# Sparse attention stage: one-hot places made between maxima and quotients, and scores multiplied ahead of the context products of two sequences back

## The reference, cut to what matters

```python
m = scores_sample.max(axis=-1) - scores_sample.mean(axis=-1)      # from 35 sampled keys
_, top_idx = jax.lax.top_k(m, TOP_U)                              # 35 queries of each head
context = broadcast(v.mean(axis=-2))                              # for every query
scores_top = einsum('bhud,bhkd->bhuk', q_top, k) * scale
attn = softmax(scores_top)
out_top = einsum('bhuk,bhkd->bhud', attn, v)
context = context.at[bi, hi, top_idx].set(out_top)
x = x + context.reshape(b, l, d) @ Wo.T + bo
```

## Time and profile before

| | us |
|---|---|
| median of 3 runs | 2660.38 (2650.34 to 2662.59) |
| the profiled execution | 2671.16, its span 2669.4 |
| PE, DVE, ACT, POOL busy in the span | 2088.6, 1658.7, 1593.7, 726.9 |
| the loop of the sparse attention, first gather to last `add` of the loop | 2114.4 to 2297.5 us from the span's start |

### The profile page before, as it was taken

The page is one execution under the profiler, slowest core; times in us unless marked ns, Lnnn a source line. Parts: engine busy times, 40 slices in busy tenths (PEclk is TensorE's granted clock), DMA queues, the critical chain, the costliest instruction groups (busy, mean ns, idle before and its releaser), DMA issues.

```text
span 2669.4 us, 47974 instructions
## 1 busy us (share of the span) xinstructions
PE 2088.6 (78%) x14951; PEld 1342.3 (50%) x14951; DVE 1658.7 (62%) x2461; ACT 1593.7 (60%) x2590; POOL 726.9 (27%) x1008
## 2 busy tenths in 40 slices
PE   6978889978889968888968888528766788836774
PEld 4444447434447434447434446416663577614663
DVE  5678847678857768857768858416324777524432
ACT  6658878658887658888658887414432244503341
POOL 0223320123320123320123312450554200171255
PEclk8979989979999979999979999759777899857876
DMA  3144400044410043410034410431111000413013
GB/s 115 36 117 120 119 14 10 14 123 116 121 32 10 11 120 117 121 38 10 11 109 121 121 39 27 93 92 29 35 40 67 28 4 1 80 50 94 14 40 121
DMA packets 104741, 172.19 MB, mean 65 GB/s; under 512 B 13792, under 2 KB 58848, under 8 KB 104288
## 3 DMA queue, kind: packets, MB, share of 16 engines
q1 hardware_dynamic: 95328, 150.66, 19.8%
q0 software_dynamic: 9216, 19.02, 2.1%
HBM read 85.19 MB, written 82.35 MB: 63 GB/s over the span
## 4 chain that ended last, share of the span: by engine, by line
PE 56%; DVE 18%; another core or an unknown queue 8%; issue 7%; ACT 4%; DMA 3%; POOL 1%; SPq 1%; DVEq 0%; ACTq 0%; POOLq 0%
DVE hmx L1935 10%; PE ps L906 10%; PE ps L872 9%; PE ps L814 2%; PE ps L715 2%; PE ps L764 2%; DMA hqk_scratch<-hqks 2%; PE ps L1306 1%; PE ps L721 1%; PE ps L1283 1%; PE ps L1231 1%; PE ps L751 1%; PE ps L752 1%; PE ps L753 1%
## 5 line engine op out<-in xcount | busy, mean ns | idle before, releaser
L1522 ACT ACTIVATE hpt<-ps 128x1024 f32<-128x1024 f32 x512 | 518.9, 1022 | 45.8 <-PE ps L893 42.8
L872 PE MATMUL ps<-hqk 24*128 24x256 f32 x2048 | 271.4, 351 | 158.1 <-DVE hmx L1935 113.1
L1935 DVE TENSOR_REDUCE hmx<-ps 128x4 f32<-128x1024 f32 x280 | 339.5, 1225 | 64.9 <-PE ps L872 57.4
L872 PEld LDWEIGHTS ps<-hqk 24*128 24x128 f32 x2048 | 163.9, 200 | 370.9 <-DVE hmx L1935 229.6
L906 PE MATMUL ps<-hpt,hvx 128*32 128x256 f32 x4096 | 285.5, 398 | 0.0
L893 PE MATMUL ps<-hqk 26*128 26x256 f32 x2048 | 266.3, 340 | 1.6 <-ACT hpt L1522 1.6
L2476 POOL DMA_INDIRECT back_scratch<-ys,xslot x160 | 153.7, 960 | 294.9 <-ACT ys L1642 255.9
L1546 ACT ACTIVATE hrow<-ps 128x512 f32<-128x512 f32 x232 | 138.5, 597 | 122.6 <-PE ps L872 122.6
L1928 DVE TENSOR_REDUCE hmx<-ps 128x2 f32<-128x512 f32 x232 | 160.7, 693 | 70.4 <-PE ps L872 70.4
L893 PEld LDWEIGHTS ps<-hqk 26*128 26x128 f32 x2048 | 158.7, 192 | 20.9 <-issue 12.2
L1944 DVE TENSOR_REDUCE hmx<-hrow 128x2 f32<-128x512 f32 x232 | 159.6, 688 | 11.0
(11 more groups left out here) (326 smaller groups left out, 5291.0 us busy)
## 6 DMA issues: line engine op xcount, KB each, us to landing
hqk_scratch<-hqks SPq DMA_DIRECT2D x64, 768.0 KB, 3.3
hqk<-hqk_scratch SPq DMA_DIRECT2D x256, 192.0 KB
slot_scratch<-filler SPq DMA_DIRECT2D x10, 1040.0 KB, 15.2
xslot<-slot_scratch SPq DMA_DIRECT2D x18, 520.0 KB
yback<-back_scratch SPq DMA_DIRECT2D x32, 256.0 KB, 5.8
mw<-mw_in SPq DMA_DIRECT2D x10, 516.5 KB, 3.6
w12raw<-w_in SPq DMA_DIRECT2D x1, 2560.0 KB, 8.8
back_scratch<-ys,xslot POOLq DMA_INDIRECT x160
```

What stands on the lines that cost most here:

```text
L872: return mm(ps[:, bank + o % 2, qt * SEQ:(qt + 1) * SEQ], hqk[r][32 * g:32 * g + 24, j, 0, qt * P:(qt + 1) * P], hqk[r][32 * g:32 * g + 24 ...
L1522: A(hpt[:, j, g:g + 2, :, :], ps[:, 2 + g:4 + g, :], ACT.Exp, scale=QSCALE).then_inc(hd_exp, 1)
L1935: V.tensor_reduce(hmx[:, r].rearrange("p t (g j) -> p g t j", j=4)[:, g:g + 2, :, j], ps[:, bank:bank + 2, :].rearrange("p x (t k) -> p x ...
```

## The change

Two orders change and nothing else: no instruction is added, removed or altered, and every wait stays with its step.

PE does scores(b) ahead of context(b-2). DVE does places(b-1) after maxima(b), just ahead of divided(b-1).

```diff
@@ PE, sparse
                     if b + 1 < BATCH:
                         project_qk(b + 1)
+                    if b < BATCH:
+                        scores(b)
                     if b >= 2:
                         context(b - 2)
-                    if b < BATCH:
-                        scores(b)
                     if b + 1 < BATCH:
                         project_v(b + 1)
                     if b >= 1:
@@ DVE, sparse
                     if b + 1 < BATCH:
                         pick(b + 1)
-                    if b >= 1:
-                        places(b - 1)
-                    if b + 1 < BATCH:
                         low(b + 1)
                     if b < BATCH:
                         maxima(b)
                     if b >= 1:
+                        places(b - 1)
                         divided(b - 1)
```

## The result

| | before, us | after, us |
|---|---|---|
| median of 12 runs | 2661.41 (2650.34 to 2669.36) | 2673.30 (2664.14 to 2680.55) |
| ratio, 95% interval | | 1.0050 (1.0032 to 1.0067) |
| the profiled execution, its span | 2671.16, 2669.4 | 2666.24, 2664.5 |

The change makes the kernel 11.9 us slower; the interval of the ratio is 8.5 to 17.8 us. The forecast was 10.3 us slower, 2670.7 us, within 2659 to 2680. The profiled execution of after happens to be a quick one (it was even quicker than that of before), so the spans of the two don't show the loss; the stage does.

The account below looks back on a forecast made before the run. Bound taken: PE's 9.30 us chain closed by some 1.8 us of DVE quotients. 13 x 0.77 + 0.3 = 10.3 us slower, added to the 2660.38 us median: 2670.7 us, range 2659 to 2680.

Parts of the forecast that it names:

- What bounds the kernel: Sparse attention round of 11.09 us: 9.30 us of PE without a gap, then some 1.8 us for DVE's quotients.
- Places behind maxima: DVE's places moved into its idle time before the quotients; `snm` 1 us earlier only adds to exps' slack: 0 us.
- The estimate of DVE's idle time before the reciprocal: Sign to check in the profile after: DVE should idle about 1.9 us before the reciprocal in a steady round.
- Scores' own needs: Scores, started earlier on PE, waits for `sqbd` only in round 15: 0.3 us once, between 0 and 0.4.
- The wait of project_v: PE's project_v waits for ACT's copy of the context in shared bank 1: 0.77 us in each of 13 rounds.
- The hand-over back to PE: Part of project_v's wait, from ACT's copy back to PE; nearest rows 0.04 and 0.14 us.
- the first product: Part of project_v's wait: 0.27 us until its first product is out, less 0.11 it adds today without a wait.
- the upper bound: High price of project_v's wait, with a restart like a gather's: 0.04 + 0.47 + 0.14 + 0.24 = 0.89 us a round.
- Values queued behind project_v: PE starts no ready matmul ahead of a waiting one, so values(b-1) is late with project_v; no separate size.
- The wait hidden: Rival: project_v's wait costs nothing, as work behind goes first or DVE is the bound; 2660 to 2661 us; chance 0.12.
- A gain from the earlier softmax: Rival: turn waits for exps, so `snm` 1 us earlier shortens some 14 rounds: 14 us less, 2646; chance 0.05.
- The clock falling once a round: Rival: two PE waits a round together lower its clock, 0.9 to 1.5 us a round: 26 us slower, 2686; chance 0.06.

Follow-up runs that it names:

- Kernel 7: Changed kernel with context(b-2), in bank 0, and out(b-3) behind values(b-1), ACT's high(b-1) before the context copy: 2451.59 us, 0.9934 of before, rounds 9.94 us.
- kernel 2: Kernel before with only DVE's order changed (places after maxima): 2466.42 us, ratio 1.0003 to before, rounds 11.10 us.
- kernel 1: Kernel before with only PE's order changed (scores ahead of context): 2477.42 us, ratio 1.0044 to before, rounds 12.00 us.
- kernel 3: Changed kernel with context products written to bank 0 instead of bank 1, same order: 2465.66 us, ratio 0.9993 to before, rounds 11.10 us.
- kernel 4: Changed kernel with ACT's copy of the context made twice: 2484.10 us, ratio 1.0061 to before, rounds 12.36 us.
- kernel 5: Kernel before with ACT's copy of the context made twice: 2466.31 us, ratio 0.9987 to before, rounds 11.10 us.
- kernel 8: As kernel 7, but DVE makes the places ahead of low and maxima, as before: 2449.74 us, ratio 0.9929 to before, rounds 9.94 us.

## Why the prediction was right

*What bounds the kernel.* Right, and it carried the rest: a chain of PE's work closed by the quotients. Kernel 7 confirms it from the other side: with context off the chain the round falls by 1.16 us, where context had 1.15.

*Places behind maxima: 0 us.* Right, shown by kernel 2. The estimate of DVE's idle time before the reciprocal, 1.9 us, was too low; it is 2.53, because places began 0.46 us earlier in the round than estimated (maxima 1.63 us without a break, `snm` 0.17 us instead of 0.38), and values ended 0.15 us later.

*Scores' own needs: 0.3 us, once.* Right: 0.25 us in round 15, the wait of the weight loads for `sqbd` that the prediction named.

*The wait of project_v: 13 times 0.77 us.* Right in place, count and mechanism (kernels 1, 3, 4, 5). The size was off: it is 0.89 by the rounds, the upper bound. Two terms were small. The hand-over back to PE was taken at 0.10 and measured 0.14. And 0.27 - 0.11 = 0.16 was allowed for the first product, where the restart measured 0.24. Both figures, 0.14 and 0.24, were known from the gather of the trace before and went into the upper bound alone. 13 x 0.12 = 1.6 us is the difference between the forecast of 10.3 and the 11.8 us of the rounds. That the medians gave 11.9 and not 9 or 15 is in part luck, given their interval.

*Values queued behind project_v.* Right: kernels 1 and 4 would not be slower otherwise. The prediction left open whether its row of round 16 shows this order, and it does not: there the last copy into `spt` ended at 2290.36 (timeline of the kernel before), after context(14) had begun. The steady rounds after do show it. The Trainium skill's rule of program order (page "TensorE: Matmul & The Clock Gate", "Step-by-step: what each phase is for") says the same, and the trace agrees: `svx` of values(b-1) was laid a round before, its `spt` was ready at 2184.42, and its matmuls began only at 2189.07, behind project_v's. The weights of project_v weren't pulled ahead of the wait either; PEld idles 0.83 us with PE [the timeline above].

*The rivals.* The wait hidden: excluded by kernel 1. A gain from the earlier softmax: excluded, since in none of the ten traces does turn wait for the exponentials after round 1, though they start anywhere from 6.6 us (kernel 7) to 8.7 us (kernel 4) into a steady round. The clock falling once a round: excluded, as the windows from 2181 to 2217 us of after have a granted clock of 1.00, and all its rounds from 3 on are alike to 0.05 us.

## What to carry to other kernels

When steps are swapped on an engine that works in order, look at what the moved step covered where it stood. Here two producers share a buffer that another engine empties between them. As soon as the two stand next to each other on the engine that bounds the kernel, each round pays for the whole evacuation, the hand-overs and the restart. Price a new wait of TensorE with the piece of chain that an existing wait shows, its restart included. And before work is moved towards the place where an idle engine waits, ask whether the engine on the chain has a gap that it could fill instead: here that turned 12 us of loss into some 15 us of gain.

## What the runs showed of the hardware

**The clock after a wait.** Every kernel waits 1.80 us ahead of gather 2, but not every execution pays for it. Kernels 2 and 5 have the same PE instructions in the same order. In kernel 5 the turn behind the wait takes 1.90 us, in kernel 2 it takes 0.99 (chain of waits; L1296 is kernel 5's turn):

```profile
2034.02 1.90 PE ps L1296 x10
```

```profile
2032.05 0.99 PE ps L1295 x10
```

The same holds for the wait of 1.94 us before context(14). Values(15) behind it takes 3.65 us in the kernel before and 2.23 in kernel 2, again with the same PE order:

```profile
2187.69 2.23 PE ps L1306 x20
```

In the profiled execution after it takes 2.23 as well, and the window has a granted clock of 1.00, where that of the kernel before had 0.81:

```profile
2289.00:2298.00 9.00, 8.19 (x48) 5.88 (x48) 3.85 (x9) 2.97 (x6) 0.00 (x0) 1.00 0.00 0
```

So each of the two places costs an execution about 1.6 us (round 2 takes 12.73 us before, where a steady round takes 11.10) or about 1.4 us, or nothing, by luck. The profiled execution before paid at both places and that after only at the first. It is the main reason why the stage of the profiled run after is only 9.9 us longer (from the first gather to out(14): 190.76 us against 180.84) where its rounds say 11.8. What decides between the two isn't shown here.

**A small VectorE instruction beside GpSimd.** The negated maxima (L2262, 5 elements per row, SBUF to SBUF) take 0.376 us as the median before and 0.172 after (one line's instructions, ns min/median/max):

```profile
L2262 DVE TENSOR_SCALAR snm<-smx x16: 172/376/377, 2122.6 to 2285.3; 112x5 f32<-112x5 f32 x16
```

```profile
L2262 DVE TENSOR_SCALAR snm<-smx x16: 171/172/375, 2109.3 to 2282.7; 112x5 f32<-112x5 f32 x16
```

Before, it starts at 2208.41, 0.12 us after GpSimd's subtraction `sxc` began (L2571, 2208.29 to 2209.22); after, at 2187.38, when GpSimd is idle until 2189.34. The ten traces have 160 of these instructions. The 63 that start 0.12 us after GpSimd's subtraction all take 0.37 to 0.38 us; the other 97 all take 0.17 to 0.18, among them 10 of kernel 8 that meet only the last 0.02 us of it. So 0.2 us go when it starts just behind the subtraction, though 0.8 us of that are still to come. What the two contend for isn't shown.

**The same kernel at 2661 and 2467 us.** The stage takes the same time in both, 11.10 us a round. The other 195 us are outside it, in the two mixtures of experts: from its first `sil` on ACT to its last, each takes 284 to 285 us in the profile of the kernel before and 171 to 172 in that of kernel 2. In the profile of the kernel before GpSimd's rows sent back (L2476) wait 294.9 us in all, 255.9 of them for ACT's `ys`; in kernel 2, with the same work there, it is 88.7 and 43.6:

```profile
L2474 POOL DMA_INDIRECT back_scratch<-ys,xslot x160 | 153.2, 958 | 88.7 <-issue 45.1 <-ACT ys L1642 43.6
```

The chains of waits say a little more. The first line is the kernel before, the second kernel 2:

```profile
PE 56%; DVE 18%; another core or an unknown queue 8%; issue 7%; ACT 4%; DMA 3%; POOL 1%; SPq 1%; DVEq 0%; ACTq 0%; POOLq 0%
```

```profile
PE 58%; DVE 20%; issue 8%; POOL 4%; ACT 4%; DMA 4%; SPq 1%; DVEq 0%; ACTq 0%; POOLq 0%
```

The 8%, some 216 us, are waits of ACT and DVE in the experts that end by nothing that the profile of this core shows, and kernel 2 has none of them. What released them isn't known. The changed kernel's own profile has them too (7%), so it is compared with the kernel before, and the experiments only within their group.
